# First part of a two-layer convolution kernel: GpSimd forms a vertical sum, VectorE counts x whole

## What is computed

```python
x = x + shift_conv(group_norm(x), theta_s, w_dw, w_pw)      # layer 0
x = x + haar_block(group_norm(x), w_c1, ..., bn2_b)         # layer 1

# layer 0, shift_conv: each channel is shifted by its own fraction of a pixel
s = z1*(1-dy)*(1-dx) + z2*(1-dy)*dx + z3*dy*(1-dx) + z4*dy*dx
s = s * w_dw[channel];  return einsum('bchw,oc->bohw', s, w_pw)
```

## Time and profile before

| | |
|---|---|
| median of three runs | 5330.59 us (5328.4 to 5332.22) |
| the profiled execution | 5333.35 us |
| its span in the profile | 5331.7 us |
| busy: PE, DVE, ACT, POOL | 87%, 87%, 81%, 22% of the span |
| mean DMA rate over the span | 289 GB/s |
| opening stage | to 97.4 us |
| images 0 to 7 of the first part | 97.4 to 2643 us |

### The profile page before, as it was taken

One profiled execution on the slowest core, in us unless ns is written; L12 is line 12 of the kernel. 1 busy time (PEld: TensorE's weight loads), 2 busy tenths in 40 slices (PEclk: granted clock), 3 DMA queues, 4 the chain that ended last, 5 costly groups with the idle time before them and its releaser, 6 DMA issues. The chain is left out here.

```text
span 5331.7 us, 54963 instructions
## 1 busy us (share of the span) xinstructions
PE 4655.7 (87%) x12634; PEld 2160.9 (41%) x12634; DVE 4621.4 (87%) x4447; ACT 4330.6 (81%) x6469; POOL 1158.6 (22%) x853
## 2 busy tenths in 40 slices
PE   2889999999999999999999999999987777777775
PEld 1334434344343443444434666666642222222222
DVE  8989899998999989999808999999468888888887
ACT  5888888888888888888837888888578888888887
POOL 0000000000000000000006888888211111111111
PEclk7999999999999999999999999999999999999998
DMA  8989999999999999999972333333159999999999
GB/s 344 364 338 374 427 396 422 426 394 427 389 425 426 394 427 392 427 391 346 361 280 96 133 135 132 133 135 135 44 120 225 236 236 236 236 236 236 236 236 223
DMA packets 248867, 1542.06 MB, mean 289 GB/s; under 512 B 29424, under 2 KB 29808, under 8 KB 91504
## 3 DMA queue, kind: packets, MB, share of 16 engines
q1 hardware_dynamic: 156528, 936.14, 44.7%
q0 software_dynamic: 36864, 268.45, 24.3%
q10 hardware_dynamic: 55296, 335.57, 15.2%
HBM read 877.35 MB, written 662.70 MB: 289 GB/s over the span
## 5 line engine op out<-in xcount | busy, mean ns | idle before, releaser
L1175 PE MATMUL ps<-arena,c2T 128*128 128x512 f32 x2048 | 1025.1, 652 | 366.3 <-ACT arena L919 363.7
L997 PE MATMUL ps<-arena 128*128 128x512 f32 x2048 | 968.3, 617 | 19.6 <-DVE small L1340 17.2
L976 PE MATMUL ps<-arena 128*128 128x512 f32 x2048 | 964.9, 598 | 7.7 <-DVE arena L1407 6.5
L972 PE MATMUL ps<-arena 128*128 128x512 f32 x1536 | 743.7, 607 | 105.7 <-ACT ps L625 49.2
L1175 PEld LDWEIGHTS ps<-arena,c2T 128*128 128x128 f32 x2048 | 401.9, 205 | 988.8 <-ACT arena L919 558.7
L919 ACT ACTIVATE arena<-ps,small 128x512 f32<-128x512 f32 x1024 | 713.0, 778 | 98.5 <-DVE arena L1618 90.4
L1502 DVE SCALAR_TENSOR_TENSOR ps<-arena,taps,ps 128x1024 f32<-128x1024 f32 (+1 forms) x602 | 655.5, 1132 | 15.6 <-PE ps L1122 13.7
L625 ACT ACTIVATE ps<-arena 128x1024 f32<-128x1024 f32 x512 | 526.4, 1028 | 161.8 <-ACT arena L666 149.1
L544 POOL TENSOR_SCALAR arena<-arena 128x256 f32<-128x256 f32 x112 | 114.7, 1029 | 2484.6 <-DMA arena<-in_x 2440.1
L666 ACT ACTIVATE arena<-ps,small 128x1024 f32<-128x1024 f32 x512 | 564.3, 1102 | 86.3 <-PE ps L976 85.7
L997 PEld LDWEIGHTS ps<-arena 128*128 128x128 f32 x2048 | 385.9, 189 | 546.1 <-issue 539.9
(11 more groups left out here) (169 smaller groups left out, 6010.4 us busy)
## 6 DMA issues: line engine op xcount, KB each, us to landing
arena<-in_x SPq DMA_DIRECT2D x508, 1024.0 KB, 12.8
out_x<-arena ACTq DMA_DIRECT2D x256, 1024.0 KB, 8.8
out_x<-arena POOLq DMA_DIRECT2D x256, 1024.0 KB, 17.0
arena<-out_x SPq DMA_DIRECT2D x208, 1024.0 KB, 15.0
y_dram<-arena ACTq DMA_DIRECT2D x128, 512.0 KB, 8.3
arena<-y_dram SPq DMA_DIRECT2D x128, 512.0 KB, 3.4
h_dram<-arena SPq DMA_DIRECT2D x112, 512.0 KB, 2.6
arena<-h_dram SPq DMA_DIRECT2D x112, 512.0 KB, 10.2
```

The source lines that it names most:

```text
L972: mm(ps[:, r, :], w_right[:, :], cells(r, 1), start=False, stop=False, skip_group_check=True)
L976: last = mm(ps[:, r, :], w_center[:, :], cells(r, 0), start=False, stop=True, skip_group_check=True)
L997: last = mm(ps[:, 4 + s % 2, :], w_c1b[:, q, :], cells[:, q // 2, q % 2, :, :], start=(q == 0), stop=(q == 3))
L1175: last = mm(ps[:, 4 * k + q, :], c2T[:, q, :], h2[:, k * HC:(k + 1) * HC], start=True, stop=True)
```

## The change

1. **GpSimd forms the first vertical sum of chunks 1, 2 and 3 of each group** (`POOL_CHUNKS`), in all images. For each it waits for the loads of slots s-1 and s and for the convolution four chunks back, then does a `tensor_scalar` (up * rows above, into u) and a `tensor_tensor` (u + rows), with a wait between them. VectorE's L1368 is left for chunk 0; for the others VectorE waits for `u_above` ahead of L1387. On GpSimd's queue the three pairs of a group stand behind `copy_top` and ahead of `copy_bottom` of it.
2. **VectorE counts whole chunks of x**: four pieces of 512, not three. `sum_x` goes from ACT, with its semaphores; `x_moments` loses a reduction and two small steps.
3. **The right neighbour is on VectorE in chunks 1 and 3** of each group in images 1 to 6 (before: 3 only), and in chunks 1, 2 and 3 in image 7 (before: 1 and 3). TensorE's L972 goes from these.
4. In image 0 the left neighbour of chunk 1 is on VectorE like the others; `w_left` goes.

```diff
+POOL_CHUNKS = (1, 2, 3)
+RIGHT_DVE = (1, SLOTS - 1)
+RIGHT_DVE_LAST = (1, 2, 3)
-DVE_PIECES = 3
+X_PIECES = 4
...
         def three_in_v(b, s):
-            return not (isinstance(b, int) and b == 0) and (s % 2 == 1 if final(b) else s == SLOTS - 1)
+            return not (isinstance(b, int) and b == 0) and s in (RIGHT_DVE_LAST if final(b) else RIGHT_DVE)
...
+            def add_above(b, g, s):
+                t = b * NCH + g * SLOTS + s
+                u = u_buf[s][:, :, 1:W + 1]
+                for near in (s - 1, s):
+                    wait_alone(pool, b * (16 * NG) + g * 16 + 16, slot_in[near])
+                wait_alone(pool, nth(t * 2 + 1, 2 * SLOTS), conv_done)
+                pool.tensor_scalar(u, ring[:, s * ROWS:(s + 1) * ROWS, :], up, 0.0, ALU.mult, ALU.add).then_inc(u_above, 1)
+                wait_alone(pool, above_made(b, g, s) - 1, u_above)
+                pool.tensor_tensor(u, u, slot(s), ALU.add).then_inc(u_above, 1)
...
             def image_rows(b):
+                group_rows(b, 0)
                 copy_bottom(b, 0)
                 with pool.Fori(1, NG - 1) as g:
                     copy_top(b, g)
+                    group_rows(b, g)
                     copy_bottom(b, g)
                 copy_top(b, NG - 1)
+                group_rows(b, NG - 1)
+
+            pool.wait_ge(setup_done, 1)
...
-                    if ahead_of:
-                        if last and s == 0:
-                            act.wait_ge(mom_ready, b * 2 + 2)
-                        if first and isinstance(b, int) and b == 0:
-                            for pair in first_pairs(s):
-                                sum_x(1, *pair)
-                        else:
-                            sum_x(*ahead_of, s)
...
-                stt(out=u, in0=ring[:, s * ROWS:(s + 1) * ROWS, :], scalar=up, in1=slot(s),
-                    op0=ALU.mult, op1=ALU.add).then_inc(u_up, 1)
+                if s not in POOL_CHUNKS:
+                    stt(out=u, in0=ring[:, s * ROWS:(s + 1) * ROWS, :], scalar=up, in1=slot(s),
+                        op0=ALU.mult, op1=ALU.add).then_inc(u_up, 1)
...
-                dve.wait_ge(u_up, t + 1)
+                if s in POOL_CHUNKS:
+                    dve.wait_ge(u_above, above_made(b, g, s))
+                else:
+                    dve.wait_ge(u_up, b * NG + g + 1)
```

More of the change, by code:

```diff
@@ L683, in square_x1 @@
                 nc.scalar.activation(squares, x1_made(s, place), ACT.Square, accum_out=total).then_inc(sq_done, 1)
[L685 to L700, removed]
             def make_y1(b, g, s):
@@ L733, in square_y1, with shift_group @@
                                      accum_out=sums_y1[:, 1, bass.ds(c, 1)]).then_inc(y1_counted, 1)
-            def shift_group(b, g, before, tail, ahead_of, place):
+            def shift_group(b, g, before, tail, place):
                 first, last = place == "first", place == "last"
@@ L770, in shift_group, with image @@
                     square_x1(b, g, s, place, chunk and chunk[0] * NCH + chunk[1] * SLOTS + chunk[2])
[L772 to L776, removed]
+            def image(b, before, tail):
+                shift_group(b, 0, before, tail, "first")
+                shift_group(b, 1, before, tail, "second")
+                shift_group(b, 2, before, tail, "")
                 with act.Fori(3, NG - 2) as g:
[L778 to L783, removed]
+                    shift_group(b, g, before, tail, "")
+                shift_group(b, NG - 2, before, tail, "held")
+                shift_group(b, NG - 1, before, tail, "last")
             square_root(1)
@@ L787, in _ @@
                 put_x(0, 0, 0, half)
-            image(0, before=False, tail=False, following=True, beyond=True)
-            image(1, before=True, tail=False, following=True, beyond=True)
-            with act.Fori(2, B - 2) as b:
-                image(b, before=True, tail=True, following=True, beyond=True)
-            image(B - 2, before=True, tail=True, following=True, beyond=False)
-            image(B - 1, before=True, tail=True, following=False, beyond=False)
+            image(0, before=False, tail=False)
+            image(1, before=True, tail=False)
+            with act.Fori(2, B - 1) as b:
+                image(b, before=True, tail=True)
+            image(B - 1, before=True, tail=True)
             for s in range(1, SLOTS):
@@ L958, in conv @@
                 k = s % 2
-                near = 1 if left_on_pe(b, s) else 0
                 def cells(r, dx):
-                    return u_buf[s][:, 2 * r:2 * r + 2, near + dx:near + dx + W]
+                    return u_buf[s][:, 2 * r:2 * r + 2, dx:dx + W]
                 for half in range(2):
                     if half == 0:
-                        if left_on_pe(b, s):
-                            pe.wait_ge(u_done, nth(t))
-                        else:
-                            pe.wait_ge(v_done, v_made(b, g, s))
+                        pe.wait_ge(v_done, v_made(b, g, s))
                     pe.wait_ge(x_in_psum, nth(t * 2 + half))
@@ L972, in conv @@
                         mm(ps[:, r, :], w_right[:, :], cells(r, 1), start=False, stop=False, skip_group_check=True)
-                    for r in range(2 * half, 2 * half + 2) if left_on_pe(b, s) else ():
-                        mm(ps[:, r, :], w_left, cells(r, -1), start=False, stop=False, skip_group_check=True)
                     for r in range(2 * half, 2 * half + 2):
@@ L1260, in count_x @@
                 for r in pieces:
-                    last = nc.vector.bn_stats(stats_x[:, bass.ds(i * (6 * DVE_PIECES) + 6 * r, 6)],
+                    last = nc.vector.bn_stats(stats_x[:, bass.ds(i * (6 * X_PIECES) + 6 * r, 6)],
                                               chunk[:, r * BANK:(r + 1) * BANK])
-                if DVE_PIECES - 1 in pieces:
+                if X_PIECES - 1 in pieces:
                     last.then_inc(x_counted, 1)
@@ L1395, in shift_rows @@
                 elif ahead_of and not late and not three_in_v(b, s):
[L1396 to L1410 removed]
+                    count_x(*ahead_of, s, range(2, X_PIECES))
+                dve.wait_ge(u_done, nth(t))
+                v, beside = u_buf[s][:, :, 0:W + 1], u_buf[s][:, :, 1:W + 2]
+                left_added = stt(out=v, in0=v, scalar=left, in1=beside, op0=ALU.mult, op1=ALU.add)
+                if three_in_v(b, s):
+                    left_added.then_inc(v_left, 1)
+                    if ahead_of and not late:
+                        count_x(*ahead_of, s, range(2, X_PIECES))
+                    dve.wait_ge(v_left, left_made(b, g, s))
+                    v = u_buf[s][:, :, 0:W]
+                    stt(out=v, in0=u_buf[s][:, :, 1:W + 1], scalar=right, in1=v,
+                        op0=ALU.mult, op1=ALU.add).then_inc(v_done, 1)
+                else:
+                    left_added.then_inc(v_done, 1)
                 if late and not final(b):
```

66 lines of the change are left out of this document (24 added, 42 removed).

## The result

The changed kernel takes **5860.6 us** (four runs, 5852.8 to 5861.4) against 5329.5 for the kernel before in the same comparison: a ratio of 1.099, 95% interval 1.098 to 1.101. The forecast was 5820 us within 5570 to 6080. The profiled execution has a span of 5859.0 us, 527 more than before.

A forecast was written before the change was run, and what follows sets the result against it. DVE and PE bound the first half of an image, transfers the second. Images 1 to 6 +348, image 0 +41, image 7 +91, opening +10 sum to +490 on 5333.35, less 2.8 to the median: 5820 us, range 5570 to 6080.

The forecast's parts named there:

- DVE and GpSimd exclude each other in SBUF, whole instruction by whole instruction: First part: two-tensor DVE steps and GpSimd instructions never overlap in SBUF; a 4.5 us sum stops DVE for its full length.
- GpSimd's prices: Per pair on GpSimd, 2048 elements: tensor_scalar 2.0 us, tensor_tensor 4.5 us; three pairs 19.5 us a group.
- 47.1 us a group: Images 1 to 6: DVE and GpSimd alternate, 45.2 + 10 x 5/11 - 2.6 us a group, between bounds 42.6 and 55.3.
- 10 x 5/11 - 2.6: Group of images 1 to 6: the part of 10 us of bn_stats not covering GpSimd, less 2.6 us saved at hand-overs.
- Images: Images 1 to 6 387 us each against 328.9, +348 together; image 0 339, +41; image 7 366, +91.
- the small steps at the borders of an image: Images 1 to 6: small steps DVE does alone, 5 us extra in the first group and 5 in the last.
- The opening stage: Before image 0: four pieces a chunk on DVE, 128 x 0.595 us from 23.5, ending at 99.7 against 89.4, +10.
- Stages two and three: After the images: the same instructions as before, so a change of 0.
- Rival A: GpSimd late: slots land 20 us after issue rather than 13.8, using up 5 us of slack; 6190 us; chance 0.08.
- Rivals B and C: B: GpSimd gives the port up inside instructions, 5258 us, chance 0.07. C: holds it for data only, about 5550, 0.10.
- Signs: Trace signs: DMA about 370 GB/s, PE under 80%, opening ending near 100 us, image 7 longer by a third.

The follow-up runs named there:

- the extra work that nobody waits for: Kernel before, plus three GpSimd tensor_scalar and tensor_tensor pairs on idle buffers in each of groups 1 to 7 of image 7: 5438.8 us, ratio 1.021.
- the halves: Changed kernel with each GpSimd tensor_tensor of 2048 elements cut into two of 1024: 5776.4 us, ratio 1.083.
- the memsets: Kernel before, plus six GpSimd memsets of 2048 elements in each of groups 1 to 7 of image 7: 5330.6 us, ratio 0.9997.
- the run with one chunk in halves: Kernel before with GpSimd forming the first sum of chunk 2 only, in halves, and the small copy as a tensor_reduce: 5383.1 us, ratio 1.010.
- Parts 2 to 4: Changed kernel with part 1 undone, so VectorE forms all vertical sums again: 5466.0 us, ratio 1.026.
- part 1 alone: Kernel before with only GpSimd forming the first sum of chunks 1 to 3: 5645.7 us, ratio 1.059.

## Why the prediction was right, point by point

- **DVE and GpSimd exclude each other in SBUF, whole instruction by whole instruction.** Shown, by the extra work that nobody waits for (image 7 +118 us where +109 was reckoned) and by the halves. What was read from border copies of 0.4 us held for sums of 4.2 us. By the Trainium skill's rule (SBUF — State Buffer, "Who interferes with whom") both the hold beside reading instructions and its absence beside memsets were to be expected; the runs agree, with 6.42 and 2.37 us for the same step.
- **GpSimd's prices.** 2.0 us for the `tensor_scalar`: 1.96 measured. 4.5 for the sum, by the slope between 896 and 1024 elements: 4.16 measured, 8% less; from 1024 to 2048 elements the slope is 1.75 ns an element, not the 2.08 read between 896 and 1024.
- **47.1 us a group.** 46.9 measured in the last groups of image 3 (its others 43.8 to 52.1). Reckoned as 35.0 of DVE's own and 12.1 of standing; over images 1 to 6 the lines above give 565 / 48 = 11.8. The six inner groups of image 3 are 46.9 in the mean as well, but they aren't alike, as the forecast had it; they run from 43.8 to 52.1 by how long DVE is held in each. That the sum came within 0.2 us is partly luck: the three pairs take 18.4 us by themselves, 1.1 less than the 19.5 put in, while what is left of 46.9 beyond the steps and GpSimd's work is 2.8 us (46.9 - 11 x 2.26 - 18.4 - 0.8), 0.9 more than the 1.9 put in (10 x 5/11 - 2.6). Image 7's inner groups are 44.9 us for 45.1 reckoned, by the same cancelling (at the forecast's 2.26 us a step): GpSimd 1.1 less, and 1.7 us saved at hand-overs instead of 2.6.
- **Images.** One term was mis-sized: images 1 to 6 took 394.0 us in the mean (452.6 to 2816.4), not 387, +42 over six. The term that was short is "the small steps at the borders of an image, which DVE does alone". I took 5 us each for the first and the last group; image 3's took 58.8 and 54.1 us, 11.9 and 7.2 over 46.9, so 9.1 more than put in. DVE doesn't do these steps alone, GpSimd holds them too. Two of their rows in images 1 to 6:

```profile
L1261 DVE TENSOR_SCALAR arena<-ones,small 128x8 f32<-128x8 f32 x48 | 21.0, 486 | 0.2
L1269 DVE SCALAR_TENSOR_TENSOR small<-small 128x1 f32<-128x1 f32 x6 | 13.5, 2244 | 0.2
```

They were 0.24 and 0.21 us in the kernel before (there L1271 and L1281). Together with L1321 (last heading), L1257 and L1289 they grew by 55 us over the six images, 9.2 an image, which is the missing amount. Image 0: 343.5 against 339; image 7: 360.8 against 366.
- **The opening stage.** DVE's one row is now

```profile
25.00 76.04 DVE L1251 BATCH_NORM_STATS2 arena<-arena 128x6 f32<-128x512 f32 x128
```

without a pause, 0.594 us a piece as in the earlier trace rows; it ends at 101.0, and the first image begins at 109.1 instead of 97.4, +11.7 where I had +10. The 128 pieces end 10.2 us later counted from their start, as reckoned; the other 1.5 us is the setup, which ended at 25.00 instead of 23.54. In the other runs it ended at 23.9 to 24.8, with and without GpSimd's work, so not all of that is the change's. Behind the pieces nothing changed: 8.0 us either way, as the L1268 aggregate takes 0.9 us more (3.62) and the reduction and the small steps that went made up for it.
- **Stages two and three.** The remaining difference of the profiled spans, 527 - 11.7 - 46.3 - 390.5 - 85.7, is -7 us; the forecast had 0. After DVE's last step of image 7 TensorE had less of a backlog: its last convolution matmul ended 9.5 us later instead of 15.0. In every run with a longer image 7 the rest is 5 to 11 us shorter than before, and with the memsets, where image 7 grew by 2 us only, it is not.
- **Rival A, GpSimd late.** It didn't come in the changed kernel. GpSimd began chunk 1 of image 3's next group at 1479.47, 5.5 us behind `u_done`, was done at 1488.98, and DVE needed it at 1504.87: 16 us of slack where I had 5. Its load landed 4.9 us after its issue; in the median loads of x take 10.7 us now, not 13.8, those of the ring by themselves 6.3 instead of 12.3. No idle time of DVE in the first part was ended by `u_above`:

```profile
DVE small L1196 <- ACT small L642: 3.6, 2, 2.4
DVE small L1275 <- PE ps L945: 1.9, 2, 1.6
```

(DVE's waits from 110 to 3170 us, whole list: total, times, longest.) A slower kernel relieved the queue that rival A feared. In the run with one chunk in halves, which is nearly as fast as the kernel before, 25 us of waits for GpSimd did come in images 1 to 6.
- **Rivals B and C** (GpSimd gives way, wholly or in part) fell with the run of extra work, steps of 6.4 us, and with the halves, whose longest step follows the length of GpSimd's instruction.
- **What the parts are worth together.** Parts 2 to 4 cost 130 us, part 1 alone 310, all 531. Most of the 90 us between lie in images 1 to 6 (65 by the traces), and there in the slack: before, DVE waited for transfers in the late groups, and more work or holds could hide there. DVE's idle time in images 1 to 6 was 134 us before, 36 with part 1 alone, 11 with parts 2 to 4 and 13 with all: the same slack can be used up once only.
- **Signs.** PE was 79% busy in images 1 to 6 (under 80% forecast), image 7 grew by 31% (a third), the opening's pieces ended at 101.0 (near 100). The DMA was at 342 GB/s over images 1 to 6 where I had said about 370, and the groups weren't alike.

## What to carry to other kernels

Before work is moved from DVE to GpSimd, count on the port and not on the engines: DVE's two-tensor SBUF steps and GpSimd's reading instructions add up (11 x 2.26 + 3 x 6.1 us here), while GpSimd's work could lie beside `bn_stats`, the small reduction and steps with a PSUM operand, and GpSimd's memsets beside two-tensor steps (not beside DVE's copies). A full engine can be a waiting one: compare the mean duration of the same form with that of a kernel without the neighbour. The price of such a rule can be read in advance from the smallest instance in the trace, here border copies whose maximum was six times their median.

## What the runs showed of the hardware that I had not expected

Small one-tensor instructions on DVE can stand behind GpSimd as long as large ones do. The `tensor_scalar` of 128x512 that makes the c1 weights, once an image, first in the kernel before, then in the changed kernel:

```profile
L1336 DVE TENSOR_SCALAR arena<-arena,small x8: 476/480/482, 436.5 to 2672.0; 128x512 f32<-128x512 f32 x8
```

```profile
L1321 DVE TENSOR_SCALAR arena<-arena,small x8: 480/4377/4378, 507.2 to 3200.7; 128x512 f32<-128x512 f32 x8
L1351 DVE COPY arena<-arena x224: 149/163/4160, 153.7 to 3170.0; 128x8 f32<-128x8 f32 x112
```

0.48 us became 4.38, and a copy of eight elements up to 4.16. The copy also stood behind GpSimd memsets (0.69 us in the mean), beside which the two-tensor steps ran free, and as a `tensor_reduce` it never stood (0.172 us at most). So these runs show two kinds of conflict, one over reading and one that, by the memsets, seems to involve writing, and which of them an instruction has goes by its form, not by its size. The Trainium skill (SBUF — State Buffer, "Who interferes with whom") lists copy and `tensor_scalar` as forms that can enter a two-port mode and `tensor_reduce` as one that never does; these three numbers agree with it. By that list the small steps at the borders of an image belonged among the held ones, where the forecast had them done alone.

TensorE's granted clock in images 1 to 6 was 0.98 to 0.99 before and is now about 0.90 of 2.4 GHz, a mean of stretches at 2.4 and at 1.2 GHz: it now waits for DVE between groups of matmuls (184 us for L1388 and 173 us for L1395 in images 1 to 6). DVE, which works ahead of it, waited for TensorE 0.4 us in images 0 to 6, so the lower clock cost nothing there.
